# Interleaving the score matmuls of four heads on TensorE in a four-layer transformer kernel

## What is computed

```
x = x + L0_attn(xn) + L0_ffn(xn)   # 16 heads of 8, rotary; top-2 of 8 experts with capacity
x = x + L1_attn(xn) + L1_ffn(xn)   # linear recurrence; 15 experts, top 3
x = x + L2_attn(xn) + L2_ffn(xn)   # 16 heads of 8, rotary; top-1 of 8 experts
x = x + L3_attn(xn) + L3_ffn(xn)   # 16 heads of 8, ALiBi and causal; gated feed-forward of 384
```

## Time and profile before

| | |
|---|---|
| median of 3 runs | 2079.53 us (2074.1 to 2083.88) |
| the profiled execution | 2077.18 us, its span 2074.8 us |
| PE busy | 1624.0 us (78%) |
| DVE busy | 1238.6 us (60%) |
| ACT busy | 766.0 us (37%) |
| POOL busy | 380.3 us (18%) |
| chain that ended last | PE 48%, DVE 19%, issue 13%, DMA 8%, POOL 7% |
| turns of layer 0 / 2 / 3 in the trace | about 125 to 625 / 1160 to 1590 / 1655 to 2065 us |

### The profile page before, as it was taken

The page is one execution under the profiler, slowest core; times in us unless marked ns, Lnnn a source line. Parts: engine busy times, 40 slices in busy tenths (PEclk is TensorE's granted clock), DMA queues, the critical chain, the costliest instruction groups (busy, mean ns, idle before and its releaser), DMA issues.

```text
span 2074.8 us, 44343 instructions
## 1 busy us (share of the span) xinstructions
PE 1624.0 (78%) x12567; PEld 1050.6 (51%) x12567; DVE 1238.6 (60%) x3512; ACT 766.0 (37%) x1723; POOL 380.3 (18%) x488
## 2 busy tenths in 40 slices
PE   3257999999972599998983588888887688888888
PEld 3123666666632577877872244444543344444444
DVE  6454666566675665665574455555557566666664
ACT  2013445445441222322230254445454144434444
POOL 1274101101167011111123300000006200000000
PEclk9855999999965698988885598999997599999999
DMA  7023455455421000000001332333232111111110
GB/s 233 28 70 101 141 155 174 137 157 174 130 58 37 0 1 1 0 0 0 0 1 40 89 95 89 98 112 110 82 95 57 36 39 42 40 40 39 37 40 15
DMA packets 133278, 144.90 MB, mean 70 GB/s; under 512 B 15001, under 2 KB 114130, under 8 KB 132946
## 3 DMA queue, kind: packets, MB, share of 16 engines
q1 hardware_dynamic: 127058, 131.37, 21.4%
q0 software_dynamic: 6144, 12.60, 2.1%
HBM read 104.65 MB, written 39.52 MB: 69 GB/s over the span
## 4 chain that ended last, share of the span: by engine, by line
PE 48%; DVE 19%; issue 13%; DMA 8%; POOL 7%; SPq 2%; ACT 2%; DVEq 1%; ACTq 0%; POOLq 0%
PE pO L694 6%; DMA stk<-packed_qk 6%; PE pT_ L557 5%; PE pH L584 5%; PE pY L592 5%; DVE X L1278 4%; PE pH L500 4%; POOL sorted_x L910 3%; PE pS L642 3%; PE pS L664 3%; DVE mx L1239 2%; PE pT_ L490 2%; PE pY L512 2%; PE pT_ L555 2%; DVE stk L1245 2%
## 5 line engine op out<-in xcount | busy, mean ns | idle before, releaser
L804 ACT ACTIVATE pex<-pT_ 128x512 f32<-128x512 f32 (+1 forms) x768 | 426.6, 562 | 656.1 <-PE pT_ L557 362.8
L1239 DVE TENSOR_REDUCE mx<-pS 128x2 f32<-128x512 f32 x512 | 348.2, 688 | 194.9 <-PE pS L540 176.8
L557 PE MATMUL pT_<-stk 32*128 32x256 f16 x1024 | 208.2, 298 | 120.0 <-DMA stk<-packed_qk 67.0
L540 PE MATMUL pS<-stk 32*128 32x256 f16 x1024 | 220.3, 304 | 23.4 <-DMA stk<-packed_qk 19.6
L694 PE MATMUL pO<-pex,va 128*9 128x256 f32 (+1 forms) x3072 | 218.4, 408 | 2.0 <-ACT pex L804 2.0
L797 ACT ACTIVATE wb<-pH,b 128x256 f32<-128x256 f32 x256 | 107.3, 470 | 268.4 <-PE pH L500 268.4
L883 POOL TENSOR_TENSOR qk<-qkf,qk 128x512 f16<-128x512 f32 x48 | 55.4, 1155 | 779.5 <-DVE qk L1211 407.3
L557 PEld LDWEIGHTS pT_<-stk 32*128 32x128 f16 x1024 | 55.9, 94 | 238.0 <-issue 87.3
L500 PE MATMUL pH<-XT,w 128*128 (+1 forms) x512 | 146.7, 413 | 0.0
L584 PE MATMUL pH<-xsT,wb 128*128 128x128 f32 x888 | 134.1, 297 | 0.0
L1245 DVE SCALAR_TENSOR_TENSOR stk<-pS,stk 128x512 f16<-128x512 f32 x96 | 66.3, 691 | 109.2 <-PE pS L664 105.0
(11 more groups left out here) (195 smaller groups left out, 2841.5 us busy)
## 6 DMA issues: line engine op xcount, KB each, us to landing
wb<-in_w SPq DMA_DIRECT2D x111, 514.0 KB, 3.8
stk<-packed_qk SPq DMA_DIRECT2D x96, 256.0 KB, 2.8
packed_qk<-qk SPq DMA_DIRECT2D x144, 128.0 KB, 2.0
xsb<-sorted_x SPq DMA_DIRECT2D x111, 64.0 KB, 3.4
sorted_y<-ysb SPq DMA_DIRECT2D x111, 64.0 KB, 3.1
sorted_x<-wb SPq DMA_DIRECT2D x2, 2048.0 KB, 13.3
w<-in_w SPq DMA_DIRECT2D x2, 1024.0 KB
out<-X SPq DMA_DIRECT2D x16, 128.0 KB, 1.8
```

The lines of the kernel that those rows point to most:

```text
L540: return pe.matmul(bank[:, part * T:(part + 1) * T], stk[rows, side, j, part * P:(part + 1) * P], stk[rows, side, j, T:2 * T], start=True, ...
L557: return pe.matmul(bank[:, part * T:(part + 1) * T], key, stk[rows, side, j, 0:T], start=True, stop=True)
L804: act.activation(pex[:, k % 8, 0:n], bank[:, 0:n], ACT.Exp).then_inc(s("T_free"), 1)
L1239: ins = dve.tensor_reduce(mx[:, :, j, col], bank.rearrange("p (c n) -> p c n", c=2), AX.X, ALU.max)
```

## The change

Two heads of a pair are issued together. In the list, T(h), T(h+1), S(h^2), S((h+1)^2) stand ahead of both heads' other steps, so the four use four different groups of 32 rows and the four banks of `pT_` and `pS`. PE waits until all four banks are free and the data is there, issues the masks of all four (layer 3), then part 0 of all four, then part 1 of all four. At turn -1 (S alone) and turn 15 (T alone) two are interleaved. Q1 moves beside Q0 and M0 waits for the S of heads 0 to 7, wherever they stand.

```diff
         frame = []
         for h in range(H):
-            frame += ([("T", h)] if here else []) + ([("S", h ^ 1)] if ahead else []) + ["F"]
+            if h % 2 == 0:
+                frame += [("T", h), ("T", h + 1)] if here else []
+                frame += [("S", h ^ 2), ("S", h + 1 ^ 2)] if ahead else []
+            frame += ["F"]
             frame += [("D", h)] if here else []
...
                 if layer == 3:
-                    frame += {LAG + 4: [("Q", 0)], LAG + 5: [("Q", 1)], LAG + 7: [("W", 0)]}.get(h, [])
+                    frame += {LAG + 4: [("Q", 0), ("Q", 1)], LAG + 7: [("W", 0)]}.get(h, [])
...
+                    elif kind in "TS" and k % 2 == 0:
+                        heads = turn.steps[at:at + (4 if here and ahead and kind == "T" else 2)]
+                        if kind == "S" and here:
+                            continue
+                        for kd, h, loc in heads:
+                            if kd == "T":
+                                if h % 2:
+                                    pe.wait_ge(s("T_free"), PRIMED + use_t + loc - 1)
+                                    if h < 8:
+                                        pe.wait_ge(s("S_free"), PRIMED + use_s - uses_behind_maxima(l, turn.n - 1))
+                                    else:
+                                        pe.wait_ge(s("S_free"), PRIMED + use_s + used_at(turn, "M", 1) + 1)
+                            elif h % 2:
+                                pe.wait_ge(s("S_free"), PRIMED + use_s + loc - 1)
+                                pe.wait_ge(s(f"spread{h // 8}"), PRIMED + turn.count(16, 32))
+                        for kd, h, loc in heads:
+                            if kd == "T":
+                                key_scores_mask(l, pT_[:, loc % 2, :])
+                            else:
+                                row_scores_mask(l, pS[:, turn.s_bank(loc), :])
+                        for part in range(2):
+                            for kd, h, loc in heads:
+                                if kd == "T":
+                                    ins = key_scores(l, par, h, pT_[:, loc % 2, :], part)
+                                else:
+                                    ins = row_scores(l, nxt, h, pS[:, turn.s_bank(loc), :], part)
+                                if part == 1:
+                                    ins.then_inc(s(f"{kd}_full"), 1)
```

More of the change, by code:

```diff
@@ L563, in take_turn @@
                 use_s, use_t, use_h, use_y, use_o = (turn.use(r) for r in "STHYO")
-                paired = False
+                here, ahead = (any(kind == what for kind, _, _ in turn.steps) for what in "TS")
                 for at, (kind, k, local) in enumerate(turn.steps):
@@ L571, in take_turn @@
                         bank = pT_[:, local % 2, :]
-                        pe.wait_ge(s("T_free"), PRIMED + use_t + local - 1)
+                        if kind != "T":
+                            pe.wait_ge(s("T_free"), PRIMED + use_t + local - 1)
                     elif kind in "GBW":
@@ L659, in take_turn @@
                     elif kind == "M":
-                        last = max(loc for kd, kk, loc in turn.steps[:at] if kd == "S") if k == 0 else -1
+                        last = max(loc for kd, kk, loc in turn.steps if kd == "S" and kk < 8) if k == 0 else -1
                         pe.wait_ge(s("S_free"), PRIMED + use_s + last + 1)
@@ L665, in take_turn @@
                         ins.then_inc(s("S_full"), 1)
[L666 to L682, removed]
                     elif kind == "O":
```

## The result

The changed kernel takes 2167.9 us (median of four runs, 2160.5 to 2171.3), against 2078.1 for the kernel before on the same chip: ratio 1.0425, interval 1.0388 to 1.0462, 90 us slower. The forecast was 2122, slower by 43. The sign was right and the time is inside the range, but the change is twice as large as forecast.

A forecast was written before the change was run, and what follows sets the result against it. PE was taken as busiest (78% against DVE's 60%), with evacuation waits added by the change. 2077.2 + 2 + 7 + 19 (layers 0, 2, 3) + 15 (edges) = 2120 us, taken as 2122 for the median; range 2075 to 2172.

The forecast's parts named there:

- The wait and its mechanism: At score pairs, PE waits until every earlier pS use is evacuated; two DVE reductions, 1.38 us, free the second bank at 1.8.
- pair 6 of layer 0: Pair 6 in layer 0 waits for J0 and J1 behind two reductions and Y0's copy: about +0.3 us.
- T6 to T8 of layer 0: Layer 0, pair 8: PE saves 0.5 us, P's 0.88 us evacuation lies ahead: 5.74 becomes 6.12 us, a loss of 0.38.
- layer 3's pair 8: Layer 3: reductions, P0 and P1 evacuations, then four masks before the scores: 4.14 us against 3.74, +0.4.
- Four groups at once: At score steps, four row groups run together: a pair's eight matmuls cost about 0.34 us, saving 0.5 us a pair.
- rival C: Score pairs in most blocks: the four groups run two by two, 58 us more, 2180 us; chance 0.06.
- Rival A: Whole kernel faster: evacuation stays hidden and PE's saving comes through, 2013 us; chance 0.12.
- layer 0, T12 to T0: End of a layer 0 turn: stays as long as before, 0 us gained; pair 14's savings become idle time.
- layer 2, pairs 2, 6, 8: Layer 2: pair 2 waits for both reductions, 6 for J1, 8 for P1: +0.3, +0.7, +0.6 us.
- layer 3, T10 to T0: End of a layer 3 turn: the 9.22 us stays and takes on the masks, +0.33 us.
- the edges: Turns -1 and 15 and thin turns 0, 1 and 14, where little covers the evacuation: taken as 15 us.
- rival B: Slower by the clock: layers 0 and 3 drop to 1.2 GHz some 3 us a turn, 40 us more, 2160; chance 0.17.

The follow-up runs named there:

- The joint wait alone: The kernel before, order and interleaving of two kept, S at even heads waiting until every earlier use of its ring is evacuated: 2295.0 us, ratio 1.1026.
- two couples: The changed kernel's list kept, each pair's four issued as two (T, S) couples, each waiting only for its own banks: 2149.2 us, ratio 1.0335.
- the four in layer 0 alone: Kernel before with the change in layer 0 only, odd heads' filling slot behind O, J, P, V, idle-filling matmuls at T0 in layers 0 and 2: 2048.5 us, 0.9851.
- the filled kernel before: The kernel before with unneeded matmuls (2, 12 and 4 in layers 0, 2, 3) ahead of T0: 2054.6 us, ratio 0.9867.

## Why the prediction was right or wrong

**The wait and its mechanism: right.** The named places are in PE's waits, P, J, V and M's subtraction. One of them cost nothing: before pair 6 of layer 0, +0.3 us was forecast and 0.0 came. T6 to T8 of layer 0 was 6.26 us where 6.12 was worked out; layer 3's pair 8 was 4.39 against 4.14. DVE's busy time did not change; the transfer wait did not shrink. The joint wait alone made the kernel before slower by 213 us. What the prediction did not see is that the new list brings this wait even without the joint issue: with two couples the second still waited for P1's evacuation, and some 69 us of the loss stayed.

**Four groups at once: right.** 0.33 us for eight matmuls, 0.34 predicted, so rival C is out. By the Trainium skill, TensorE: Matmul & The Clock Gate, section Part 3: Packing small matmuls, four row groups were measured at 3.07 times one; the trace agrees as far as it goes, with twice the matmuls in the time that two groups took. What one group alone takes no run here shows. Rival A, which needed the evacuation to stay hidden as well, fell: PE was busy 106 us less and the kernel was slower.

**The terms at full clock, in us a turn:**

| | predicted | measured |
|---|---|---|
| layer 0, pairs 2, 4, 6, 8, 10, 12 | +0.4 -0.5 +0.3 +0.38 +0.1 -0.5 | +0.24 -0.51 0.0 +0.50 +0.16 -0.64 |
| layer 0, T12 to T0; turn | 0; +0.2 | 0.0; -0.3 |
| layer 2, pairs 2, 6, 8 | +0.3 +0.7 +0.6 | +0.54 +0.94 +0.78 |
| layer 2, pairs 4, 10, 12 | -0.4 to -0.5 twice, -0.1 | -0.51 -0.34 0.0 |
| layer 2, T12 to T0; turn | 0; +0.5 | 0.0; +1.4 |
| layer 3, pairs 2, 4, 6, 8, 10 | (none) +0.2 +0.2 +0.4 +0.1 | +0.05 +0.29 +0.35 +0.65 +0.07 |
| layer 3, T10 to T0; turn | +0.33; +1.2 | +0.47; +1.9 |

Times 12, 13 and 15 turns, the measured column gives -4, +18 and +29 us, together 43. The waits of the whole kernel are 56, which leaves 13 for the edges, where 15 stood. So the waits came to 56 us against a forecast that was 43 in all (2 + 7 + 19 for the turns, 15 for the edges). Layer 2 was sized too small by 0.9 us a turn. Up to 0.3 of it is that I took its turn of before as it stood, though some of it ran at 1.2 GHz: T0 to T2 is 1.3 us at full clock and was taken as 1.6. The rest lies in pairs 6 and 8, where the waits were longer by 0.2 us each, and in savings that were smaller by some 0.1 at pairs 10 and 12. Layer 3 was sized too small by 0.7, of which pair 8 is 0.25.

**The step that failed: the clock.** The prediction treated it as rival B, an alternative to the forecast at 0.17 and +40 us, and its sum has no term for the clock. But B's cause is the forecast's own result: the same sums put more idling into every turn, about 1.8 us at T0 of layer 0 by the prediction's own words. The two add: 43 + 40 = +83 by the prediction's own prices (rival B's 2160 us), against +90. Measured, the clock is 34 us, about 19 in layer 0, where the kernel before has 3 of the kind, and 17 in layer 3 (the sum of what their turns are over the full-clock one); layer 2 fell to 1.2 GHz before as well and pays the same 2 us a turn in both kernels. That B reached both layers 0 and 3 was right as priced; its chance was not.

In layer 3 B was right for half of its reason: it looked to T0, and there three of the eleven falls lie; the other eight lie behind T6 and T10, in the stretch shown above behind a wait for DVE. The Trainium skill, TensorE: Matmul & The Clock Gate, section A second HAM failure mode: psum-queue depth-cycling, describes something of this kind, a clock that oscillates because PE idles between groups of matmuls while it goes round its banks. The trace agrees (0.50 behind a 1.85 us wait for DVE), though here it is one wait and not many small ones. The same page's section Loop structure matters more than you think notes, of a loop whose next matmuls follow immediately, that a copy out of PSUM by VectorE does not break PE's warmth; here the next matmuls waited for the evacuation, and the clock fell behind that wait.

**Open:** the edges, 13 us by difference, were not tried by themselves. About half of them show in the traces: from the last T0 of layer 2 to the first of layer 3 it is 70.8 us before, 77.6 changed, and 71.2 with the two couples, which at turns -1 and 15 are issued singly. How much four groups save by themselves is not known. Whether the four in layer 0 alone beat the filled kernel before (0.9851 against 0.9867) is not settled.

## What to carry to other kernels

Ask of every packing what it makes the engine wait for: a step that fills four banks at once, or a list that puts them next to each other, turns double buffering into a wait for all of them. Here the wait alone cost 213 us in the old order, the new list without packing cost some 69, and four groups at once did not win it back. A saving on the busiest engine counts only in the stretches which that engine fills; work out each distance against the other engine's time for it first. Where a forecast adds idling to every turn, the clock belongs into the sum and not among the rivals, and a baseline's turn must be read at full clock before it is compared.

## What was not expected

Filling PE's idle time with multiplications that nobody needs made the unchanged kernel 1.3% faster (0.9867, again 0.9874 on another chip), and no reordering tried here was clearly better than that. Layer 2's turn went from 28.0 to 29.9 us down to 26.8. And the clock fell in the midst of layer 3's turns, behind a wait for DVE of 1.85 us, where no transfer was late.
